# GELU statistics as scaled fp16 high and low sums, their products in the second QKV bank in head 13, and two input scalings moved to head 8

## What is computed

```python
def bitlinear(x, w):
    xn = layer_norm(x)            # (x - mean) / sqrt(var + EPS), over the last axis
    w_hat = ternarize_weights(w)  # sign(round(w / (gamma + EPS))) * gamma
    return jnp.einsum('bsd,od->bso', xn, w_hat)   # forward value, up to the activation clip
h = bitlinear(x, w_fc)            # 512 -> 2048
h = jax.nn.gelu(h, approximate=False)
return bitlinear(h, w_proj)       # 2048 -> 512
```

## Time and profile before

| | us |
|---|---|
| median of 3 runs | 1116.39 |
| lowest and highest | 1112.8 and 1116.63 |
| the profiled execution | 1117.71 |
| its span on the core | 1115.6 |
| PE busy | 1056.1 (95%) |
| DVE busy | 858.7 (77%) |
| ACT busy | 808.4 (72%) |
| POOL busy | 542.9 (49%) |

### The profile page before, as it was taken

How to read it: one execution, slowest core, us unless ns; L and a number is a source line. 1 busy time by engine, 2 the same in 40 slices (tenths; PEclk the granted TensorE clock), 3 DMA queues, 4 the chain that set the end, 5 groups by cost and what they waited for, 6 DMA issues and landing times.

```text
span 1115.6 us, 24332 instructions
## 1 busy us (share of the span) xinstructions
PE 1056.1 (95%) x9428; PEld 668.6 (60%) x9428; DVE 858.7 (77%) x1623; ACT 808.4 (72%) x1372; POOL 542.9 (49%) x358
## 2 busy tenths in 40 slices
PE   4757899999999999999999999999999999999898
PEld 1334555666666665666666576666656666666555
DVE  3679758787787878787796878878687887878646
ACT  4787675867768586877868687786858687685944
POOL 0622282744729183563809264471917456290703
PEclk8969899999999999999999999999999999999989
DMA  8811213122131323113131312213131311112100
GB/s 328 324 47 29 72 25 77 58 55 65 30 90 44 77 59 81 58 25 78 44 95 44 77 58 44 64 38 95 44 77 58 65 62 35 42 40 57 58 20 20
DMA packets 79618, 76.99 MB, mean 69 GB/s; under 512 B 8848, under 2 KB 60048, under 8 KB 78992
## 3 DMA queue, kind: packets, MB, share of 16 engines
q1 hardware_dynamic: 79504, 75.45, 24.1%
HBM read 41.72 MB, written 8.40 MB: 45 GB/s over the span
## 4 chain that ended last, share of the span: by engine, by line
PE 88%; ACT 5%; DVE 4%; issue 1%; DMA 0%; POOL 0%; SPq 0%; ACTq 0%; DVEq 0%
PE F L838 10%; PE F L839 10%; PE F L679 9%; PE F L681 9%; PE QB L647 3%; PE QA L647 3%; PE QB L648 3%; PE QB L649 3%; PE QA L648 3%; PE QA L649 3%; PE T L876 3%; PE SA L736 2%; PE SB L736 2%; PE PV L753 2%; PE PV L752 2%; PE PV L751 2%
## 5 line engine op out<-in xcount | busy, mean ns | idle before, releaser
L838 PE MATMUL F<-yT_hi,fc_t 128*128 128x256 f16 x1024 | 228.7, 275 | 0.0
L839 PE MATMUL F<-yT_lo,fc_t 128*128 128x256 f16 x1024 | 228.3, 274 | 0.0
L606 POOL TENSOR_TENSOR rqk<-ssq,half 128x16 f32<-128x16 f32 x64 | 192.5, 3014 | 62.0 <-DVE ssq L1317 62.0
L679 PE MATMUL F<-proj_t,hs 128*128 128x512 f16 x512 | 194.1, 379 | 0.0
L681 PE MATMUL F<-proj_t,hs 128*128 128x512 f16 x512 | 193.8, 378 | 0.0
L575 POOL TENSOR_TENSOR acc<-acc,hg 128x512 f32<-128x512 f32 x96 | 150.0, 1562 | 16.0 <-ACT hg L980 2.8
L1283 DVE SCALAR_TENSOR_TENSOR hs<-hg,g_inv,hs 128x512 f16<-128x512 f32 x128 | 104.9, 820 | 65.1 <-ACT hs L985 64.7
L980 ACT ACTIVATE hg<-F,g_fc 128x512 f32<-128x512 f32 x128 | 87.3, 682 | 51.6 <-PE F L839 51.6
L575 POOL TENSOR_TENSOR acc<-hg 128x512 f32<-128x512 f32 x16 | 20.3, 1268 | 211.4 <-ACT hg L980 183.5
L582 POOL TENSOR_TENSOR acc<-acc,hq 128x512 f32<-128x512 f32 x90 | 114.2, 1268 | 13.3 <-ACT hq L1042 5.1
L569 POOL TENSOR_TENSOR rs<-var,half 128x1 f32<-128x1 f32 x32 | 17.6, 550 | 206.5 <-DVE var L1163 206.5
(11 more groups left out here) (206 smaller groups left out, 2724.3 us busy)
## 6 DMA issues: line engine op xcount, KB each, us to landing
stk<-qkT SPq DMA_DIRECT2D x128, 128.0 KB, 2.5
xtok<-in_x SPq DMA_DIRECT2D x17, 512.0 KB, 3.8
xT_sb<-in_xT SPq DMA_DIRECT2D x16, 512.0 KB, 3.5
stk<-qkT SPq DMA_DIRECT2D x128, 64.0 KB, 2.1
xres<-in_x SPq DMA_DIRECT2D x15, 512.0 KB, 3.6
out<-xres SPq DMA_DIRECT2D x15, 512.0 KB, 2.8
stk<-in_w_emb SPq DMA_DIRECT2D x4, 512.0 KB, 4.8
fc_t<-in_w_qkv SPq DMA_DIRECT2D x2, 1024.0 KB, 10.9
```

Of the source, the lines that this page charges most:

```text
L606: pool.tensor_tensor(rqk[:, n % 2, :], ssq[:, n % 2, :], half[:, :], ALU.pow).then_inc(rqk_r, 1)
L679: pe.matmul(FB[t][:, :], hs[:, 0, k // 2, col:col + P], proj_t[:, k, :], start=(k == 0), stop=False)
L838: pe.matmul(dst, w, yT_hi[:, k, :], start=(k == 0), stop=False)
L839: mm = pe.matmul(dst, w, yT_lo[:, k, :], start=False, stop=(k == KT - 1))
```

## The change

The four fp32 products become eight fp16 ones. After the fold, in head 11, ACT writes `acc_hi`, the fp16 high part of `accf` scaled by 1/gamma (values) and 1/(256 gamma^2) (squares), two operations of 256 columns. In head 12 DVE writes `acc_lo`, the rest, two operations of 256 columns. In head 13, after the transpose of piece 3, PE multiplies both parts by a constant fp16 column (1/2048 and 256/2048), into the first four columns of QB; so it waits for the last `qkn`, and the value projection into QB in head 15 waits until DVE has copied the result (`mean_r`). DVE's three small operations move from head 12 to head 13, POOL's power to head 13, `c1` and `c2` to head 15. The input scalings of parts 0 and 1 move from head 12 to head 8. Steps 15 and 16 keep bank `T` for the statistics.

```diff
-           11: ("piece", 2), 12: ("stats", 0), 13: ("piece", 3), 15: ("heads", 2)}
-FOLD_AT, RMS_AT, RS2_AT, STAT_AT, OUT1_AT = 10, 3, 12, 14, 15
+           11: ("piece", 2), 13: ("piece", 3), 15: ("heads", 2)}
+LAST_TURN_AT = {6: ("heads", 0), 10: ("heads", 1), 13: ("stats", 0), 15: ("heads", 2)}
+FOLD_AT, RMS_AT, RS2_AT, STAT_AT, OUT1_AT = 10, 3, 13, 15, 15
+HIGH_SUM_AT, LOW_SUM_AT, MEAN_AT = 11, 12, 13
+SQ_DOWN = 256.0
...
-SCALE_AT = {12: (0, 1), 13: (2, 3)}
+SCALE_AT = {8: (0, 1), 13: (2, 3)}
...
+            pool.memset(mean16[:, 0:1], 1.0 / F).then_inc(c_pool, 1)
+            pool.memset(mean16[:, 1:2], SQ_DOWN / F).then_inc(c_pool, 1)
...
+                    if t == 1 and k == 0 and ffn is not None:
+                        pe.wait_ge(mean_r, nth(ffn, 1, 1))
...
-                    if kind == "stats" and ffn is not None:
-                        pe.wait_ge(fold_r, nth(ffn, 1, 1))
-                        open_turn(("stats", 0))
+                    if h == MEAN_AT and ffn is not None:
+                        pe.wait_ge(sumlo_r, nth(ffn, 2, 2))
+                        if qkv is None:
+                            open_turn(("stats", 0))
+                        else:
+                            pe.wait_ge(qkn_r, nth(qkv, 4, 4))
                         for s in range(2):
                             for t in range(TT):
-                                mm = pe.matmul(T[:, s * TT + t:s * TT + t + 1], accf[:, s, t * P:(t + 1) * P],
-                                               ones[:, 0:1], start=True, stop=True)
-                        mm.then_inc(turned, 1)
+                                dst, rows = mean_bank(qkv)[:, s * TT + t:s * TT + t + 1], slice(t * P, (t + 1) * P)
+                                pe.matmul(dst, acc_hi[:, s, rows], mean16[:, s:s + 1], start=True, stop=False)
+                                mm = pe.matmul(dst, acc_lo[:, s, rows], mean16[:, s:s + 1], start=False, stop=True)
+                        mm.then_inc(turned if qkv is None else mean_done, 1)
...
+                    if h == HIGH_SUM_AT and ffn is not None:
+                        act.wait_ge(fold_r, nth(ffn, 1, 1))
+                        for s, scale in ((0, g_inv), (1, g_sq)):
+                            act.activation(acc_hi[:, s, :], accf[:, s, :], ACT.Identity, scale=scale[:, 0:1]
+                                           ).then_inc(sumhi_r, 1)
...
+                    if h == LOW_SUM_AT and ffn is not None:
+                        for s, scale in ((0, g_inv), (1, g_sq)):
+                            dve.wait_ge(sumhi_r, nth(ffn, 2, s + 1))
+                            if s == 0:
+                                dve.wait_ge(fold_r, nth(ffn, 1, 1))
+                            dve.scalar_tensor_tensor(acc_lo[:, s, :], accf[:, s, :], scale[:, 0:1], acc_hi[:, s, :],
+                                                     ALU.mult, ALU.subtract).then_inc(sumlo_r, 1)
...
+                    if h == MEAN_AT and ffn is not None:
+                        if qkv is None:
+                            dve.wait_ge(turned, turn(i, ("stats", 0)) + 1)
+                        else:
+                            dve.wait_ge(mean_done, nth(ffn, 1, 1))
...
+                        dve.tensor_copy(st[:, :, :].rearrange("p s t -> p (s t)"), mean_bank(qkv)[:, 0:2 * TT]
+                                        ).then_inc(unturned if qkv is None else mean_r, 1)
```

More of the change, by code:

```diff
@@ L155, in turn_at @@
 def turn_at(i):
+    if isinstance(i, int) and i >= B - 1:
+        return LAST_TURN_AT
     return FIRST_TURN_AT if isinstance(i, int) and i == -1 else TURN_AT
@@ L177, in turn_uses @@
     _, ffn, att, qkv, pre = stages(i)
-    runs = {"y": ffn, "stats": ffn, "max": att, "heads": att, "piece": qkv, "rms": pre}
+    runs = {"y": ffn, "stats": ffn if qkv is None else None, "max": att, "heads": att, "piece": qkv, "rms": pre}
     if pre is not None and not early(pre):
@@ L245, in adaln_ffn_kernel @@
         g_both = sb("g_both", [P, 1])
+        g_sq = sb("g_sq", [P, 1])
+        eps_s = sb("eps_s", [P, 1])
+        mean16 = sb("mean16", [P, 2], F16)
         colsum = sb("colsum", [P, D])
@@ L287, in adaln_ffn_kernel @@
         accf = sb("accf", [P, 2, N])
+        acc_hi = sb("acc_hi", [P, 2, N], F16)
+        acc_lo = sb("acc_lo", [P, 2, N], F16)
         st = sb("st", [P, 2, TT])
@@ L397, in adaln_ffn_kernel @@
         fold_r = sem("fold_r")
+        sumhi_r = sem("sumhi_r")
+        sumlo_r = sem("sumlo_r")
+        mean_done = sem("mean_done")
+        mean_r = sem("mean_r")
         st2_r = sem("st2_r")
@@ L443, in score_bank, with mean_bank @@
             return banks[h % len(banks)]
+        def mean_bank(qkv):
+            return T if qkv is None else QB[1]
         def residue(b):
@@ L450, in nothing @@
             pass
-        C_POOL = 7
+        C_POOL = 9
         block = ctx.enter_context(nc.Block())
@@ L1057, in _ @@
             act.wait_ge(s_gk, 1)
-            run(iteration, lambda: qkv_weights((0, 1)), nothing, lambda: act.wait_ge(s_gam, 7))
+            run(iteration, lambda: qkv_weights((0, 1)), nothing, lambda: act.wait_ge(s_gam, 9))
         @block.vector
@@ L1128, in proj_magnitude @@
                 dve.reciprocal(g_inv[:, :], gam[:, 0:1]).then_inc(s_gam, 1)
-                dve.scalar_tensor_tensor(g_both[:, :], gam[:, 0:1], -1.0, gam[:, 1:2], ALU.mult, ALU.mult
-                                         ).then_inc(s_gam, 1)
+                dve.tensor_scalar(g_both[:, :], gam[:, 1:2], -1.0, None, ALU.mult).then_inc(s_gam, 1)
+                dve.wait_ge(s_gam, 6)
+                dve.tensor_scalar(g_sq[:, :], g_inv[:, :], g_inv[:, 0:1], 1.0 / SQ_DOWN, ALU.mult, ALU.mult
+                                  ).then_inc(s_gam, 1)
+                dve.tensor_scalar(eps_s[:, :], g_inv[:, :], g_inv[:, 0:1], EPS, ALU.mult, ALU.mult).then_inc(s_gam, 1)
             def last_weights():
-                dve.wait_ge(s_gam, 7)
+                dve.wait_ge(s_gam, 9)
             def input_lo(b, k):
@@ L1324, in iteration @@
                                           ).then_inc(qkn_r, 1)
+                    if h == MEAN_AT and ffn is not None:
[3 more added lines that the diff above has]
+                            dve.wait_ge(mean_done, nth(ffn, 1, 1))
+                        if live(ffn - 1):
+                            dve.wait_ge(c_r, nth(ffn - 1, 2, 2))
+                        dve.tensor_copy(st[:, :, :].rearrange("p s t -> p (s t)"), mean_bank(qkv)[:, 0:2 * TT]
+                                        ).then_inc(unturned if qkv is None else mean_r, 1)
+                        if qkv is None:
+                            dve.wait_ge(unturned, turn(i, ("stats", 0)) + 1)
+                        else:
+                            dve.wait_ge(mean_r, nth(ffn, 1, 1))
+                        dve.tensor_tensor(st2[:, :], st[:, 0, :], st[:, 0, :], ALU.mult).then_inc(st2_r, 1)
+                        dve.wait_ge(st2_r, nth(ffn, 1, 1))
+                        dve.scalar_tensor_tensor(var2[:, :], st[:, 1, :], eps_s[:, 0:1], st2[:, :], ALU.add, ALU.subtract
+                                                 ).then_inc(var2_r, 1)
                     kind, n = turn_at(i).get(h, (None, 0))
@@ L1342, in iteration @@
                                                      ALU.mult, ALU.mult).then_inc(u_r if k < KT - 1 else unturned, 1)
[L1343 to L1353, removed]
                     if h == FOLD_AT and ffn is not None:
@@ L1370, in iteration @@
                         dve.wait_ge(rs2_r, nth(ffn, 1, 1))
-                        dve.tensor_scalar(c1[:, :], st[:, 0, :], g_inv[:, 0:1], None, ALU.mult).then_inc(c_r, 1)
+                        dve.tensor_copy(c1[:, :], st[:, 0, :]).then_inc(c_r, 1)
                         dve.tensor_scalar(c2[:, :], rs2[:, :], g_both[:, 0:1], None, ALU.mult).then_inc(c_r, 1)
```

## The result

| | before | after |
|---|---|---|
| median, us | 1116.39 (1112.8 to 1117.73) | 1128.72 (1128.36 to 1130.59) |
| profiled execution | 1117.71 | 1130.4 |
| its span | 1115.6 | 1128.6 |

The ratio after to before is 1.0124, with a 95% interval of 1.0103 to 1.0146: the changed kernel is slower by 12.3 us on the medians, where 11.1 was forecast.

The account below looks back on a forecast made before the run. PE was taken as the bound, busy 63.88 of 63.95 us a step, with DVE close behind. 0.7 us in 14 middle steps (9.8), 0.7 in step 15 and 0.6 in step 16 made +11.1: median 1127.5, range 1113 to 1134.

Parts of the forecast that it names:

- The slot in head 12: PE, head 12: the 1.00 us slot of eight fp32 statistics instructions before the scores of head 13 goes away.
- eight products take 0.21: PE, before the scores of head 14: eight one-column fp16 products add 0.21 us, upper bound 1.00.
- delays `p_hi` of head 12: ACT: the high part of piece 2 waits for the fold and two added operations, so `p_hi` starts 1.27 us late.
- The transpose of piece 3: PE: waits some 1.5 us for the late `qkn`, so this transpose comes 0.47 us later than before.
- The scores of head 14: PE, behind the transpose of piece 3 and the new products: 0.68 us late.
- The last step: Step 16: the old slot becomes a chain of high sums, low sums and products, some 1.7 us against 1.1, 0.6 more.
- The scalings in head 8: DVE, head 8: two scalings of 0.79 to 0.88 us fit into idle time and cost nothing if their factor is there.
- rival C: Head 8: scalings wait for their late factor; a landing 1 us later adds about 0.8 us a step, 1138; chance 0.06.
- a new wait in head 8: Sign of a wrong forecast: a new wait in head 8 or 9, where no DVE wait for the DMA was expected.
- DVE's wait of over 1 us before `p_lo` of head 12: Sign expected in the profile after: DVE waits over 1 us before `p_lo` in head 12.
- Rival A: PE gets its slot back: each step loses 0.79 us, median 1104, or 1104 to 1110 if only in part; chance 0.15.
- by the same chain: Step 15: the same two ACT operations, in a stretch bound by ACT and DVE, cost 0.7 us.

Follow-up runs that it names:

- e10: The changed kernel with POOL forming the input factor in head 1 instead of head 3: ratio 1.0122 to the kernel before, median 1128.97 us.
- e1: The changed kernel with ACT's two high-part operations (`acc_hi`) in head 12 behind `p_hi`, instead of head 11: ratio 0.9966 to the kernel before, median 1111.24 us.
- e7: e1 with DVE's tail reordered, `result` behind the last `o_sb` and `residual` behind the last `v_lo`: ratio 0.9941 to the kernel before, median 1109.11 us.
- e9: e7 with POOL forming the input factor in head 1 instead of head 3: ratio 0.9932 to the kernel before, median 1107.65 us.
- e4: The changed kernel with ACT's two high-part operations behind piece 2's high part, still in head 11: ratio 1.0073 to the kernel before, median 1123.39 us.
- e5: The changed kernel with DVE's two low-part operations (`acc_lo`) behind `qkn` in head 12: ratio 1.009 to the kernel before, median 1124.91 us.

## Why the prediction was right

By its own steps, against the trace after:

- The slot in head 12 is gone, and eight products take 0.21: exact, at under 0.03 each. The 81 ns of the Trainium skill (TensorE: Matmul & The Clock Gate, Back-to-back issue gap), which would have given 0.65, is its figure for products of 128 columns; for 1 to 64 columns the same section has an issue floor of about 25 ns, 0.20 for eight. The rows agree with the floor.
- ACT waits for the fold and delays `p_hi` of head 12 (forecast 1.27): `p_hi` starts 3.06 behind the transpose of piece 2, 1.84 before the change, so 1.22 late. The high sums measure 0.82 from the first to the next operation, forecast 0.85; the low sums 0.79, forecast 0.84.
- The transpose of piece 3 was put 0.47 late and is 0.28 late. The high and the low sums were put a little too long, and the way from `qkn` to the transpose, put at 0.15, was 0.05 (499.36 to 499.41).
- The scores of head 14: 0.50 late, forecast 0.68. The step then loses a further 0.20 in DVE's tail, which I had not kept apart from PE's delay. The two errors nearly cancel, and that is luck: 0.70 to 0.75 a step, forecast 0.7.
- The last step, in the chain of waits of each kernel, from the start of the fold to the next product: 2.56 (1116.80 to 1119.36) against 1.80 (1104.56 to 1106.36), +0.76, forecast 0.6.
- The scalings in head 8 do fit, with 0.18 us to spare, and rival C, which had 0.06 as a main cause, exists in the small: one step of fourteen. Taken to the letter, the sign of being wrong "a new wait in head 8" is met in that one step; it cost 0.4 us.
- Of the other signs, most came as told: ACT waits 0.52 for `accf`, PE 1.14 for `qkn`, a step takes 64.70. DVE's wait of over 1 us before `p_lo` of head 12 came in two parts, 0.85 one operation earlier and 0.48 there. PE's busy time is 4.3 us lower and not 10: a part of its waiting counts as busy, and a low clock in step 0, told in the last section, adds to it in this execution; in e10, without that, it is 7.1 lower.
- Rival A, that relief of the engine of highest occupancy shows in the step, was not what came of this order of the queues, and is what e1 and e7 show: the same relief pays once the other engines' order lets it. Its price of 0.79 a step was not reached in e9 either, which has 0.63. The Trainium skill's rule behind it (Perfetto Trace Analysis, Identifying the Most-Contended Engine) agrees with e1 and not with the changed kernel; for TensorE that section judges headroom by the busy share of the weight loads, here 60%, and not by that of the matmuls, which rival A went by.

Of the 13.0 us between the two spans, 11.1 lie in steps 1 to 14, where the forecast had 9.8: 14 times 0.75 makes 10.5, and single longer steps add the rest. From the DMA of step 15 (1036.91 before, 1049.04 after) to the last fold it is 0.1, where step 15 was to lose 0.7 "by the same chain"; that term failed. Counted from the fold of step 15, `p_lo` of head 12 is 1.13 late there, but `rden` behind it only 0.13, since DVE had waited 1.25 us for PE ahead of `rden` in the kernel before. The last step adds 0.8. The remaining 1.1 lie ahead of step 1, for which the forecast had nothing: 2.0 more in step 0, with a low clock in that one execution (see below), and 1.0 less in the setup. So the forecast's 11.1 lacks 2.5 us in three places and has 0.6 too much in a fourth, and the total is nearer than its terms.

## What to carry to other kernels

When a saving on the full engine is paid for with small operations on its suppliers, price the place in the queue and not the duration: 0.8 us of work behind the instruction that the full engine needs cost nothing, and the same 0.8 us ahead of it, with a wait for a result that was not ready, turned a gain of 0.46 us a step into a loss of 0.75. Look for idle time that lies ahead of the needed result; idle time behind it does not hide work that stands ahead of it. And when the full engine's stream gets shorter, read at once which engine arrives at the joint next, since here it stood 0.2 us behind.

## What was not expected of the hardware

Two rows with a price that no term had. In the changed kernel's step 0, whose only edit is the place of two scalings, the time grows from 73.25 to 75.27 us. The busy time by stretch shows a granted clock of 0.74 and 0.83 there, where the kernel before has 1.00, and the 512-column products stand 0.43 us apart instead of 0.21, the lower of the two levels:

```profile
107.00:111.00 4.00, 3.27 (x32) 1.64 (x33) 2.92 (x7) 0.60 (x1) 0.00 (x0) 0.74 0.71 137
111.00:115.00 4.00, 4.00 (x24) 1.79 (x23) 1.62 (x5) 1.92 (x5) 0.00 (x0) 0.83 0.78 152
```

In e1, e4 and e10, with the same step 0 as the changed kernel or all but the same, it takes 73.3 to 73.4 us, so this is that execution's and not the kernel's. PE had idled before it: the products of probabilities and values wait 1.57 us for `p_lo` just ahead. But the same wait, 1.57 to 1.58 us, stands in e1, e4 and e10, where the clock behind it is 1.00; what decided between them is not shown.

And in e5 one late factor cost far more than its wait. The timeline of DVE, then the busy time of the stretches behind it:

```profile
810.56 2.63 DVE L1414 SCALAR_TENSOR_TENSOR xT_sb<-xT_sb,cur_a,rx_all 128x256 f32<-128x256 f32 x2 [1.65 <-DMA rx_all<-rx_row]
```

```profile
812.00:816.00 4.00, 2.09 (x19) 1.30 (x20) 3.97 (x8) 1.25 (x4) 0.91 (x1) 0.81 0.00 0
816.00:820.00 4.00, 4.00 (x41) 2.76 (x40) 2.50 (x5) 2.97 (x6) 3.29 (x1) 0.76 0.00 0
```

DVE waited 1.65 us, the two scalings took 2.63 instead of 0.87, PE waited 2.98 us for `o_sb`, and the granted clock fell to 0.81 and 0.76; the step took 67.87 us instead of 64.34. A wait of 1.65 us became a loss of 3.5, with a lower clock after PE had idled; how much of the loss is the clock's was not separated, nor why the scalings themselves ran so long.
